# Two transformer layers on one core: late conditioning products, and maxima and exponentials over two banks at once

## The reference

```
layer 0: mod = silu(cond) @ ada_w + ada_b  -> shift, scale, gate for attention and for the MLP
  x += gate_sa * (attention(LN(x)*(1+scale_sa)+shift_sa) @ sa_proj_w + b)
  x += attention(LN(x), context, key mask) @ ca_proj_w + b
  x += gate_ff * (gelu((LN(x)*(1+scale_ff)+shift_ff) @ fc1 + b) @ fc2 + b)
layer 1: three adaptive layer norms, gamma, beta = cond @ ln_w[k].T + ln_b[k]
  self attention with RoPE, cross attention with RoPE, gelu MLP, each added to x
```

## Time and profile before

| | |
|---|---|
| median of three runs | 1737.17 us |
| the profiled execution's own time | 1736.45 us |
| its span, first to last instruction | 1734.6 us |
| mean granted TensorE clock | 0.970 |

### The profile page before, as it was taken

The page is one execution under the profiler, slowest core; times in us unless marked ns, Lnnn a source line. Parts: engine busy times, 40 slices in busy tenths (PEclk is TensorE's granted clock), DMA queues, the critical chain, the costliest instruction groups (busy, mean ns, idle before and its releaser), DMA issues.

```text
span 1734.6 us, 45297 instructions
## 1 busy us (share of the span) xinstructions
PE 1523.8 (88%) x17760; PEld 1321.9 (76%) x17760; DVE 1118.1 (64%) x2628; ACT 965.1 (56%) x2009; POOL 720.2 (42%) x983
## 2 busy tenths in 40 slices
PE   6779989898998989999897998989899898998987
PEld 5668878777787877878786786877778787786866
DVE  3456756566665656666666776666776676776654
ACT  1556565665656566565664655556555565655543
POOL 1342424224243332424546546454554545546421
PEclk9989999999999999999998999999999999999989
DMA  6010010101001010101110100000000000000000
GB/s 216 27 50 2 15 50 15 50 9 44 14 15 50 13 53 9 44 14 38 44 41 29 38 14 26 11 29 8 19 14 14 26 11 16 15 13 14 2 13 13
DMA packets 33968, 49.43 MB, mean 28 GB/s; under 512 B 3456, under 2 KB 24896, under 8 KB 33760
## 3 DMA queue, kind: packets, MB, share of 16 engines
q1 hardware_dynamic: 33760, 46.54, 8.5%
HBM read 38.07 MB, written 8.45 MB: 27 GB/s over the span
## 4 chain that ended last, share of the span: by engine, by line
PE 73%; DVE 11%; ACT 6%; issue 5%; POOL 3%; DMA 0%; SPq 0%; DVEq 0%; POOLq 0%; ACTq 0%
PE score L622 7%; PE score_t L640 7%; PE p_unit L704 6%; PE p_mix L679 6%; PE p_unit L516 6%; PE p_unit L517 5%; PE p_unit L518 5%; DVE neg_max L1062 5%; PE p_out L516 4%; PE p_out L517 3%; PE p_out L518 3%; PE p_out L668 2%; PE p_turn L687 2%; PE p_mix L547 2%; PE score_t L516 2%
## 5 line engine op out<-in xcount | busy, mean ns | idle before, releaser
L1062 DVE TENSOR_REDUCE neg_max<-score 128x4 f32<-128x512 f32 x448 | 288.2, 686 | 171.8 <-PE score L622 156.0
L622 PE MATMUL score<-k_t,q_t 32*128 32x256 f32 x1792 | 267.2, 417 | 92.8 <-POOL q_t L1310 36.6
L640 PE MATMUL score_t<-q_less,k_t 32*128 32x128 f32 x3584 | 276.5, 295 | 0.7 <-ACT probs_t L931 0.7
L622 PEld LDWEIGHTS score<-k_t,q_t 32*128 32x128 f32 x1792 | 169.3, 194 | 132.3 <-issue 86.2
L931 ACT ACTIVATE probs_t<-score_t 128x512 f32<-128x512 f32 x336 | 182.5, 595 | 122.8 <-PE score_t L640 108.6
L640 PEld LDWEIGHTS score_t<-q_less,k_t 32*128 32x128 f32 x3584 | 231.8, 197 | 10.4 <-issue 6.1
L850 ACT ACTIVATE xt<-p_mix,mod_now 128x128 f32<-128x128 f32 x384 | 154.8, 457 | 139.2 <-PE p_mix L547 137.6
L1263 POOL TENSOR_TENSOR xt_lo<-xt,xt_hi 128x256 fp32r<-128x256 f32 x128 | 93.8, 732 | 325.8 <-ACT xt_hi L855 325.8
L704 PE MATMUL p_unit<-w_out,heads_t 128*128 128x256 f32 x512 | 145.6, 407 | 30.4 <-ACT heads_t L944 29.5
L516 PE MATMUL p_out<-w_hi,hid_lo 128*128 128x256 f32 x512 | 149.6, 292 | 15.7 <-issue 8.3
L518 PE MATMUL p_out<-w_hi,hid_hi 128*128 128x256 f32 x512 | 143.1, 279 | 0.0
(11 more groups left out here) (153 smaller groups left out, 4297.1 us busy)
## 6 DMA issues: line engine op xcount, KB each, us to landing
ctxt<-in_ctxT SPq DMA_DIRECT2D x16, 512.0 KB, 3.8
side<-gates SPq DMA_DIRECT2D x15, 512.0 KB, 5.6
x_new<-in_x SPq DMA_DIRECT2D x32, 128.0 KB, 2.0
x_mid<-xs SPq DMA_DIRECT2D x8, 512.0 KB, 3.4
x_new<-x_mid SPq DMA_DIRECT2D x32, 128.0 KB, 2.0
out<-xs SPq DMA_DIRECT2D x8, 512.0 KB, 2.9
k_t<-in_L_f_wT SPq DMA_DIRECT2D x2, 1024.0 KB, 5.3
k_t<-in_ln_wT SPq DMA_DIRECT2D x2, 512.0 KB, 7.8
```

Source lines behind the costliest of these rows:

```text
L622: mm = pe.matmul(score_bank(b, r)[:, t * 2 * N:(t + 1) * 2 * N].rearrange("p (e n) -> p e n", e=2), q_t[s][rows(r), t, tokens], k_t[s][row ...
L640: mm = pe.matmul(turned_bank(b, r)[:, x * N:(x + 1) * N], k_t[s][rows(r), t, e, tokens], q_less[rows(r), j % 2, t, e, :], start=True, stop ...
L1062: dve.tensor_reduce(by_half[:, :, 2 * r:2 * r + 2, 0], score_bank(b, r)[:].rearrange("p (t e n) -> p t e n", t=CT, e=2), AX.X, ALU.max, ne ...
```

## The change

1. **Late products.** Gates, MLP modulation and bias product move from steps -11 and -8 to steps 2, 3 and 4 of group 0, all three into the bank `p_turn`, each after VectorE has read the one before; layer 1's modulations move from step -9 to step 11, into `p_out`. The rows that VectorE makes of them move to steps 2, 3, 4 and 12.
2. **Loads.** `cond` is loaded first and has a semaphore of its own. The constants that the start waits for are 7, and of `ada_w` only its first third. The other parts, `gate_bias`, `bias_rows`, output weights, fourth chunk, one ln weight and the RoPE tables are issued behind the first three weight chunks and the context; two ln weights are issued at step -7 of group 0 behind the gates' way through DRAM, into other buffers. SyncE's queue waits at that place for the gates, which are made at step 2 now; behind it stand the loads of steps 0 to 24, context and x of group 1 first.
3. **Weight split.** The low part of chunk 1 is made by VectorE (step -4) and no longer by GpSimd; the high parts of chunks 1 and 2 move one step, to -4 and -2.
4. **Two banks at once.** The two banks of a round are one tile of 1024 columns. One instruction takes the maxima of both r, one the exponentials of both; the semaphores `scored`, `scored_t`, `max_made` and `exps_made` count half as fast. The two value copies of a unit become one of 512 columns.

The tables of units and MLP parts now exist once per layer, with the same contents as before.

```
-MOD_FF_AT, MOD_LN_AT, BIAS_AT, GATE_ROWS_AT, MOD_ROWS_AT, BIAS_ROWS_AT = -11, -9, -8, -7, -6, -5
-FIRST_HI_AT = {-5: 1, -1: 2, 5: 3}
-FIRST_LO_POOL_AT = {-4: 1, 0: 2}
-FIRST_LO_DVE_AT = {-10: 0, 6: 3}
...
+GATES_AT, MOD_FF_AT, BIAS_AT, MOD_LN_AT, MOD_ROWS_AT = 2, 3, 4, 11, 12
+FIRST_HI_AT = {-4: 1, -2: 2, 5: 3}
+FIRST_LO_POOL_AT = {-2: 2}
+FIRST_LO_DVE_AT = {-10: 0, -4: 1, 6: 3}
...
-        lnw = [spare[3][:, m * CT * 2 * D:(m + 1) * CT * 2 * D].rearrange("p (t n) -> p t n", t=CT)
-               for m in range(2)] + [q_t[1][:]]
-
-        score = [bank("score0"), bank("score1")]
-        score_t = [bank("score_t0"), bank("score_t1")]
+        lnw = [w.rearrange("p b c -> p (b c)").rearrange("p (t n) -> p t n", t=CT) for w in (side[:, 1], x2)] + [ln3_w[:]]
...
+        score = bank_pair("score")
+        score_t = bank_pair("score_t")
         p_mix = bank("p_mix")
         p_turn = bank("p_turn")
         p_unit = bank("p_unit")
         p_out = bank("p_out")
-        up_ring = score_t + score
-
-        def score_bank(b, r):
-            return (score_t if b == 0 and r >= 2 else score)[r % 2]
-
-        def turned_bank(b, r):
-            return (score if b == GB - 1 and r >= 2 else score_t)[r % 2]
-
-        p_mod, p_gate = score
-        p_mod_ln, p_bias = score_t
+        up_ring = [score_t[:, 0], score_t[:, 1], score[:, 0], score[:, 1]]
...
+        def score_banks(b, h):
+            return score_t if b == 0 and h == 1 else score
+
+        def turned_banks(b, h):
+            return score if b == GB - 1 and h == 1 else score_t
+
+        p_mod = score[:, 0]
+        p_gate = p_bias = p_mod_ff = p_turn
+        p_mod_ln = p_out
...
+            ada_w = a["L0_xcond_ada_w"].rearrange("(t p) n -> t p n", p=P)
+            sp.dma_start(cond[:], a["condT"].rearrange("(t p) b -> p t b", p=P)).then_inc(cond_loaded, 16)
...
-                (cond[:], a["condT"].rearrange("(t p) b -> p t b", p=P)),
-                (ada[0], a["L0_xcond_ada_w"][0:P]),
-                (ada[1], a["L0_xcond_ada_w"][P:2 * P]),
                 (bias_mod[:], a["bias_mod"]),
-                (gate_bias, a["gate_bias"].partition_broadcast(B)),
                 (ident[:], a["ident"]),
                 (head_mask[:], a["head_mask"]),
                 (one_row[:], a["one_row"]),
-                (cos_t[:], a["cos_t"]),
-                (sin_t[:], a["sin_t"]),
-                (bias_rows[:], a["bias_rows"].partition_broadcast(P)),
                 (bias_cols[:], a["bias_cols"]),
                 (bias_v[:].rearrange("p s t -> p (s t)"), a["bias_v"]),
                 (mask_cols_u8[:], a["mask_cols"]),
             ):
                 sp.dma_start(dst, src).then_inc(c_loaded, 16)
+            for c in range(CT):
+                sp.dma_start(ada[c][:, 0:2 * D], ada_w[c, :, 0:2 * D]).then_inc(ada_loaded, 16)
...
+                                sp.wait_ge(mod_full, 3)
                             else:
                                 sp.wait_ge(gated_sa, group * 4)
                             load_gate(0, gate_sa.rearrange("p b c -> p (b c)"), group, gate_sa_loaded)
+                            if group == 0:
+                                load_ln(0)
+                                load_ln(1)
...
             load_weights(0, 0, stage, w_loaded)
-            for m in range(3):
-                sp.dma_start(lnw[m], a["ln_wT"][m].rearrange("(t p) n -> p t n", p=P)).then_inc(ln_loaded, 16)
+            load_weights(0, 1, stage, w_loaded)
+            load_ctx(0)
+            load_weights(0, 2, stage, w_loaded)
+            for c in range(CT):
+                sp.dma_start(ada[c][:, 2 * D:6 * D], ada_w[c, :, 2 * D:6 * D]).then_inc(ada_rest_loaded, 16)
+            sp.dma_start(gate_bias, a["gate_bias"].partition_broadcast(B)).then_inc(rows_loaded, 16)
+            sp.dma_start(bias_rows[:], a["bias_rows"].partition_broadcast(P)).then_inc(rows_loaded, 16)
             load_heads_out(0, SELF)
             load_heads_out(0, CROSS)
-            load_weights(0, 1, stage, w_loaded)
-            load_weights(0, 2, stage, w_loaded)
-            load_ctx(0)
-            sp.wait_ge(mod_full, 4)
             load_weights(0, 3, stage, w_loaded)
+            load_ln(2)
+            sp.dma_start(cos_t[:], a["cos_t"]).then_inc(tables_loaded, 16)
+            sp.dma_start(sin_t[:], a["sin_t"]).then_inc(tables_loaded, 16)
             body()
...
-                    pe.wait_ge(gates_made if h == 0 else bias_added, 1)
+                    pe.wait_ge(mod_step, 1)
                 elif b == 0:
-                    pe.wait_ge(exps_made, group * 32 + 4 * j)
+                    pe.wait_ge(exps_made, group * 16 + 2 * j)
                 else:
-                    pe.wait_ge(max_made, group * 32 + 4 * j + 2 * h - (2 if b == 1 and h == 0 else 0))
+                    pe.wait_ge(max_made, group * 16 + 2 * j + h - (1 if b == 1 and h == 0 else 0))
...
-                        if t == CT - 1:
-                            mm.then_inc(scored, 1)
+                    if t == CT - 1:
+                        mm.then_inc(scored, 1)
...
+                if j == 4:
+                    if group:
+                        pe.wait_ge(out_moved, group * 4)
+                    else:
+                        pe.wait_ge(mod_step, 10)
...
+                if group == 0 and j == 0:
+                    pe.wait_ge(bias_added, 1)
...
-                    if t == MOD_FF_AT:
-                        modulation((4, 3), p_mod_ln, 12)
+                    if t == GATES_AT:
                         gate_products()
+                    elif t == MOD_FF_AT:
+                        pe.wait_ge(gates_made, 1)
+                        modulation((4, 3), p_mod_ff, 0)
                     elif t == MOD_LN_AT:
+                        pe.wait_ge(queries_less, 4)
                         modulation_ln()
                     elif t == BIAS_AT:
                         bias_products()
...
             def gate_products():
+                pe.wait_ge(ada_rest_loaded, 16 * CT)
...
             def bias_products():
+                pe.wait_ge(mod_step, 3)
...
+                    dst = v_pad[s][:, 2 * half:2 * half + 2, 0:H * VW].rearrange("p b (h w) -> p b h w", h=H)[:, :, :, 0:HD]
+                    act.copy(dst, p_unit[:].rearrange("p (b h d) -> p b h d", b=2, h=H)).then_inc(values_made, 1)
...
-            def exps(group, s, b, r):
+            def exps(group, s, b, h):
                 j = 4 * s + b
-                act.wait_ge(scored_t, group * 32 + 4 * j + r + 1)
-                if r == 0 and not (group == 0 and j < 2):
+                act.wait_ge(scored_t, group * 16 + 2 * j + h + 1)
+                if h == 0 and not (group == 0 and j < 2):
                     act.wait_ge(mixed, group * 8 + j - 1)
-                if r == 0 and j < 2 and group == 0:
-                    act.wait_ge(w_lo_pool, 1 + j)
-                dst = probs_t[j % 2][:, r].rearrange("p x n -> p (x n)")
+                if h == 0 and j < 2 and group == 0:
+                    act.wait_ge(w_lo_dve if j == 0 else w_lo_pool, 2 - j)
+                dst = probs_t[j % 2][:, 2 * h:2 * h + 2].rearrange("p r x n -> p (r x n)")
+                src = turned_banks(b, h)[:].rearrange("p r n -> p (r n)")
                 if layer_of(group) == 0 and s == CROSS:
-                    op = act.activation(dst, turned_bank(b, r)[:], ACT.Exp, bias=mask_now[:, b:b + 1])
+                    op = act.activation(dst, src, ACT.Exp, bias=mask_now[:, b:b + 1])
                 else:
-                    op = act.activation(dst, turned_bank(b, r)[:], ACT.Exp)
+                    op = act.activation(dst, src, ACT.Exp)
...
-            def row_max(group, s, b, r):
+            def row_max(group, s, b, h):
                 j = 4 * s + b
-                dve.wait_ge(scored, group * 32 + 4 * j + r + 1)
-                if r == 0 and not (group == 0 and j < 2):
+                dve.wait_ge(scored, group * 16 + 2 * j + h + 1)
+                if h == 0 and not (group == 0 and j < 2):
                     dve.wait_ge(max_turned, group * 8 + j - 1)
-                by_half = neg_max[:, j % 2].rearrange("p t (c w) -> p t c w", w=HD)
-                dve.tensor_reduce(by_half[:, :, 2 * r:2 * r + 2, 0],
-                                  score_bank(b, r)[:].rearrange("p (t e n) -> p t e n", t=CT, e=2),
+                by_half = neg_max[:, j % 2].rearrange("p t (r e w) -> p r t e w", e=2, w=HD)
+                dve.tensor_reduce(by_half[:, 2 * h:2 * h + 2, :, :, 0],
+                                  score_banks(b, h)[:].rearrange("p r (t e n) -> p r t e n", t=CT, e=2),
                                   AX.X, ALU.max, negate=True).then_inc(max_made, 1)
...
-                    elif t == GATE_ROWS_AT:
-                        dve.wait_ge(mod_full, 3)
+                    elif t == GATES_AT:
+                        dve.wait_ge(rows_loaded, 32)
+                        dve.wait_ge(mod_full, 2)
```

(25 more changed lines are left out.)

158 lines of the change are left out of this document (86 added, 72 removed).

## The result

The changed kernel takes 1716.9 us in the median of four runs (1712.0 to 1722.0), beside 1735.8 for the kernel before: a ratio of 0.9892, 95% interval 0.9857 to 0.9927. It is faster, by 19 us, where 9 to 11 were forecast; direction and range held. The profiled execution is the slowest of the four, 1721.97 us with a span of 1720.1.

The account below looks back on a forecast made before the run. The prediction took the kernel as mostly TensorE work in fixed order (73% of the chain). Head -20.4 and return +15.6 give -4.8, joined instructions -5.0: 1736.45 becomes 1726.6, forecast 1726.5 us, range 1707 to 1741.

Parts of the forecast that it names:

- Direction and range: Whole kernel: faster than before, chance 0.57, with a time between 1707 and 1741 us.
- the two parts that I had named: Head with the return of its moved products, -4.8 us; joined two-bank instructions, -5.0 us.
- They keep their length, since the clock was at 2.4 GHz where they stood: Products moved from the head into group 0 take as long there: gates 3.55, MLP modulation and bias 3.41 each, layer 1's 10.08.
- 15.6 us: Cost of the moved products in group 0: gates 0, MLP modulation and bias product +6.8, layer 1's modulations +8.8.
- The head's gain of 20.4: Start of the kernel: first unit at 22.5 us, 20.4 earlier than 42.94; bounds 19 to 21.5.
- my 13.0: Head: landing time in us of the first weight chunk's load, issued at about 7.5; bounds 11.9 and 14.4.
- Two banks at once, -5.0: Score rounds: joined maxima -4 (68 pairs by 0.06 us), exponentials -1, value copies 0; bounds -16 and +1.
- The term of -1 for the exponentials: ScalarE: one joined masked pair in each of layer 0's 8 groups is on the chain, -1 us together.
- Rival 1: Half-clock stretch of 3.4 us goes in 8 of 16 groups, -14 us more: 1713; chance 0.20.
- Rival 3: Second half-clock stretch in each group, at step 3 of its scores, 27 us for 16 groups: 1753; chance 0.12.
- Rivals 2 and 4: First: joined instructions gain nothing, 1731 (1737 if head returns all), chance 0.20. Second: moved products stay hidden, 1711, chance 0.06.
- What would show it: Profile signs: first unit at 21 to 24 us, first scores 19 to 21.5 earlier, joined maxima 1.22 to 1.25, step-11 block over 10.

Follow-up runs that it names:

- the second profile: The changed kernel, unaltered, run and profiled again beside the kernel before on another chip: ratio 0.9880.
- the split kernels: Changed kernel with maxima, exponentials and value copies in two instructions again (1729 us, 0.9963), or all but the maxima, or all but the exponentials.

## Why the prediction was right, and where it was wrong

**Direction and range** came out right by the two parts that I had named, and the head alone is worth what I said: 6 us measured, 4.8 forecast. That the size came out so near is luck: two errors cancel.

**"They keep their length, since the clock was at 2.4 GHz where they stood"** is the step that failed. I took a granted clock of 1.00 at the head as a reading, while it was the absence of one. TensorE had done nothing until 16 us, and its products of 16 took 3.41 us against 1.8 at full clock. The hint was in the same trace: a first unit of 256-column products every 0.12 us beside 32-column ones every 0.21 (10.08 for 48). The Trainium skill ("TensorE: Matmul & The Clock Gate", section What's actually happening) states that "the default state is throttled, and activity releases the throttle". The runs agree on the default, and with unused products in front the records of 2.4 GHz begin at 6.1 us. But in the kernel before TensorE was busy with the small products for 22.0 of the 22.3 us from 19.7 to 42.0, and the clock rose only then. Where they stand now, the products take 2.1 us (gates), 1.9, 1.9 and 6.3 (the block), 12.2 together and not 20.45. So they did not cost 15.6 us. Group 0 grew by 7.8 in the one profile and 3.4 in the other.

**The head's gain of 20.4** was too large in part for the same reason: the first unit, at full clock before, now ran at half clock. The start of group 0 came 15.0 us earlier (17.6 in the second profile). Of the 5.4 us missing, 2.2 are the chunk's landing at 15.2 against my 13.0. I had counted only the bytes ahead of it, and not those issued behind it; that these delay it is not shown. The landing itself scatters: issued at 7.4 us in ten profiles of this head, the chunk landed between 12.8 and 15.2, so my 13.0 is inside the scatter and a part of the 2.2 is chance. 1.4 are the first unit's 12 products at 0.21 in place of 0.12 with their fill. The rest lies between the second unit and the start of group 0, where the clock fell from 31.8 to 38.6 us in this profile and not in the second.

**Two banks at once, -5.0** was mis-sized: measured -12.3. The price of the instruction was right to 0.02 us, but the step from 68 pairs at 0.06 us to -4 was wrong for layer 1. In layer 0 the joins gave 0.3 us a group between two profiles, as forecast, though the scatter is larger than that. In layer 1 they gave 1.75. I had read the pairs in a layer 0 stretch only the earlier trace rows and multiplied. There was no row of GpSimd beside VectorE in my rows, so the collision was not in the sum, nor in the rivals. The term of -1 for the exponentials is not measurable (1728.2 against 1729.0).

**The Trainium skill's rule** ("Perfetto Trace Analysis", section Optimizing Scalar/DVE Operations) on breaking instructions up would have made it no gain. It did not hold here, where the two halves are ready together: the joins gained.

**The rivals.** Rival 1 has nearly the right time, 1713, by a mechanism that did not happen: the mean clock of the groups is 0.97 to 0.98 as before. Rival 3, which gives stretches a second place, was there in part: layer 0 of the first profile lost 7.4 us of busy time to a lower clock and so gave back all of its 5.5 us of idle time. Rivals 2 and 4 fell with the split kernels: 1729 is not 1711, and 1716.7 is not 1729. **What would show it**: maxima, exponentials and gates as told. The first unit at 25.3 was outside my 21 to 24, the first scores (36.2 against 51.5) came 15.4 us earlier and not 19 to 21.5, and the block took 6.3 in place of 10 us. A group of layer 1 changed by over a microsecond, which I had named as a sign that I am wrong. It was one.

## What to carry to other kernels

- Where a trace has no clock record yet, take TensorE's clock from the pitch of its products against the same products later. Work moved from a cold head into a busy stretch may cost half its length, and removing it leaves the head cold.
- Where VectorE and GpSimd both work between SBUF buffers, price a shorter VectorE instruction by who starts first behind it, in each layer of the kernel by itself. In this kernel a saving of 0.07 us was worth 1 us at one place, and nothing that could be measured in layer 0.
- Try small products in pieces between other work, and not in one block (here 89.2 to 91.7 us against 92.1 to 96.9 for group 0). Check a few per mille of gain in several executions: the same instructions took 615.7 and 621.1 us in two kernels.

## What the runs showed that I had not expected

- The granted clock can fall while TensorE is busy without a gap. It did so during 32-column products of the changed kernel (busy 6.50 of 6.50 us from 71.9 to 78.4, clock 0.83 in that stretch), and what follows ran at 0.50 until 82.9:

```profile
71.90:78.40 6.50, 6.50 (x51) 6.50 (x50) 1.02 (x3) 0.81 (x2) 1.25 (x3) 0.83 0.12 34
78.40:83.00 4.60, 4.60 (x19) 4.13 (x19) 2.44 (x8) 1.21 (x3) 2.02 (x3) 0.50 0.00 0
```

- A maximum over two PSUM banks in one instruction takes 1.223 us, one over a single bank 0.686, so the second bank costs 0.54.
- Executions of the changed kernel spread over 11 us (1711 to 1722), and two profiles of it differ by 10.9: 2.6 at the start of group 0, 4.4 in group 0, 3.2 in groups 1 to 7. With the ln products in three parts three profiles have group 0 at 89.2 to 89.4 us (the fourth at 91.7).
